# Second attention of a two-layer kernel: value products issued in twos, maximum tiles placed anew between them

## What is computed

```python
q, k, v = proj(wq, bq), proj(wk, bk), proj(wv, bv)      # (B, 16, L, 8), L = 1024
scores = jnp.einsum('bhqd,bhkd->bhqk', q, k) / np.sqrt(HEAD_DIM)
attn = jax.nn.softmax(scores + bias[None], axis=-1)     # bias by relative position
out = jnp.einsum('bhqk,bhkd->bhqd', attn, v)
```

## Time and profile before

| | us |
|---|---|
| median of 3 runs (lowest, highest) | 2570.04 (2569.20, 2572.35) |
| the profiled execution | 2569.28 |
| its span, first to last instruction | 2567.5 |
| TensorE matmuls busy | 2312.1 (90%) |
| VectorE busy | 1850.8 (72%) |
| ScalarE busy | 1497.5 (58%) |
| TensorE busy with attends, L1360 | 267.7 |
| VectorE busy with maxima, L1462 | 605.2 |
| ScalarE busy with exponents, L1444 | 506.2 |

### The profile page before, as it was taken

How to read it: one execution, slowest core, us unless ns; L and a number is a source line. 1 busy time by engine, 2 the same in 40 slices (tenths; PEclk the granted TensorE clock), 3 DMA queues, 4 the chain that set the end, 5 groups by cost and what they waited for, 6 DMA issues and landing times. The chain is left out here.

```text
span 2567.5 us, 46435 instructions
## 1 busy us (share of the span) xinstructions
PE 2312.1 (90%) x17339; PEld 1338.3 (52%) x17339; DVE 1850.8 (72%) x2346; ACT 1497.5 (58%) x2293; POOL 125.4 (5%) x256
## 2 busy tenths in 40 slices
PE   3799999999999999999999955859999999999998
PEld 2466666666565666666566632624444444444444
DVE  8677777777777777777777775067777777777781
ACT  3465666657575656666575731306666566566666
POOL 0100000000000000000000021000000000000000
PEclk8899999999999999999999977959999999999999
DMA  2000000000000000000000008033111110112000
GB/s 75 1 0 0 0 0 0 0 0 0 0 0 0 0 0 0 0 0 0 0 0 0 0 17 194 11 45 63 18 18 20 34 26 18 27 19 32 12 2 10
DMA packets 41099, 41.16 MB, mean 16 GB/s; under 512 B 21392, under 2 KB 33632, under 8 KB 40864
## 3 DMA queue, kind: packets, MB, share of 16 engines
q1 hardware_dynamic: 38904, 36.87, 7.2%
q10 hardware_dynamic: 1448, 1.61, 0.4%
q0 software_dynamic: 640, 1.15, 0.4%
HBM read 26.60 MB, written 11.63 MB: 15 GB/s over the span
## 5 line engine op out<-in xcount | busy, mean ns | idle before, releaser
L1462 DVE TENSOR_REDUCE nm_half<-slot 128x2 f32<-128x1024 f32 x512 | 605.2, 1223 | 188.4 <-PE slot L1311 146.2
L1444 ACT ACTIVATE pT<-slot 128x1024 f32<-128x1024 f32 x512 | 506.2, 1027 | 332.0 <-PE slot L1394 278.7
L573 ACT ACTIVATE probT<-slot 128x1024 f32<-128x1024 f32 x192 | 171.0, 890 | 326.9 <-PE slot L474 326.9
L474 PEld LDWEIGHTS slot<-ident,prob 128*128 128x128 f32 x2304 | 245.7, 141 | 198.6 <-issue 166.8
L610 DVE TENSOR_REDUCE negmax<-slot 128x1 f32<-128x896 f32 (+7 forms) x416 | 282.5, 708 | 76.4 <-PE slot L464 76.4
L474 PE MATMUL slot<-ident,prob 128*128 128x128 f32 x2304 | 328.0, 281 | 2.1
L486 PE MATMUL yspace<-probT,v_sb 128*64 128x512 f32 (+3 forms) x1536 | 318.3, 507 | 0.0
L1306 PE MATMUL slot<-ks,qs 48*128 48x512 f32 x1024 | 254.3, 495 | 53.6 <-DMA ks<-rows 29.1
L565 ACT ACTIVATE prob<-slot,negmax 128x896 f32<-128x896 f32 (+7 forms) x416 | 292.6, 720 | 9.6 <-DVE negmax L610 9.6
L1360 PE MATMUL yspace<-pT,v 128*32 128x512 f32 x2048 | 267.7, 604 | 1.7 <-ACT y_raw L1431 0.8
L459 PE MATMUL slot<-k_hi,q_st 128*128 128x512 f32 (+3 forms) x608 | 240.8, 396 | 26.4 <-ACT prob L565 11.4
(11 more groups left out here) (240 smaller groups left out, 3007.8 us busy)
## 6 DMA issues: line engine op xcount, KB each, us to landing
qs<-q_hi SPq DMA_DIRECT2D x64, 64.0 KB
qs<-q_lo SPq DMA_DIRECT2D x64, 64.0 KB
ks<-k_hi SPq DMA_DIRECT2D x60, 64.0 KB
ks<-k_lo SPq DMA_DIRECT2D x60, 64.0 KB
x_tok<-in_L_attn_x_dram SPq DMA_DIRECT2D x4, 512.0 KB, 7.4
q_hi<-qk_out SPq DMA_DIRECT2D x4, 512.0 KB, 3.2
q_lo<-qk_out SPq DMA_DIRECT2D x4, 512.0 KB, 4.1
k_hi<-qk_out SPq DMA_DIRECT2D x4, 512.0 KB, 4.2
```

Of the source, the lines that this page charges most:

```text
L474: last = nc.tensor.transpose(ps[:, a * BANK + j * P:a * BANK + (j + 1) * P], prob[a][:, p_at(4 * c + j, kt)], ident[:, :])
L1444: nc.scalar.activation(pT[hp][m % PT_DEEP][:, :, :], slot[at["x", n] % RING][:, :].rearrange("p (j t) -> p j t", t=BANK), ACT.Exp)\
L1462: nc.vector.tensor_reduce(nm_half[:, h, :, p * TPB + i], slot[pos % RING][:, :].rearrange("p (a t) -> p a t", t=BANK), AX.X, ALU.max, nega ...
```

## The change

The two lists are replaced, and maximum tasks that were split around an attend now all stand ahead of it:

```diff
-                M_BEFORE = [1, 1, 1, 3, 0, 1, 1, 1, 1, 1, 1, 0, 1, 0, 1, 0, 0, 2, 2, 1, 1, 0, 1, 2, 2, 2, 2, 1, 2, 0, 0, 0]
-                AV_BEFORE = [0, 0, 0, 1, 0, 0, 1, 0, 0, 1, 0, 1, 0, 1, 0, 1, 0, 1, 1, 1, 0, 0, 0, 0, 1, 1, 1, 0, 1, 0, 0, 0]
+                M_BEFORE = [1, 2, 2, 0, 1, 1, 1, 0, 2, 0, 1, 1, 1, 1, 1, 1, 3, 0, 1, 1, 1, 1, 1, 1, 1, 1, 2, 1, 1, 1, 0, 0]
+                AV_BEFORE = [0, 0, 0, 0, 0, 0, 0, 0, 2, 0, 2, 0, 0, 0, 0, 0, 2, 0, 2, 0, 0, 0, 2, 0, 0, 0, 2, 0, 0, 0, 0, 0]
...
                             if not last:
-                                next_maxima(m_before(n)[:1])
+                                next_maxima(m_before(n))
                             for m in av_before(n):
                                 attend(m)
-                            if not last:
-                                next_maxima(m_before(n)[1:])
```

## The result

The changed kernel takes 2674.53 us (median of 4 runs, 2671.98 to 2680.13) against 2569.62 us for the kernel before in the same comparison: a ratio of 1.041, 95% interval 1.0398 to 1.0423. The forecast was 2623 us with a range to 2655. The sign was right, the size was not: +105 us in place of +53.

The account below looks back on a forecast made before the run. TensorE was taken as the bound, with new waits on the three-slot PSUM ring outweighing the pairs' saving. Twelve ordinary quads +45.7, three batch-end quads +8.4, last quad -1.3: +52.8 on 2569.3, plus 0.8, gives 2623 us, range 2596 to 2655.

Parts of the forecast that it names:

- half-clock case: Clock halves from m11 to the end of A5 in each quad: 4 us more a quad, near 2680 us; chance 9%.
- dense stretch: x10 to m18, between the second and third attend pairs: 7.97 us for 5.05 us of TensorE's work, 2.9 us waiting.

Follow-up runs that it names:

- m_only: Against the kernel before, only the maxima are placed as in the changed kernel; attends stand singly at their old places, three in the tail: 2641.6 us, ratio 1.0288.

## What to carry to other kernels

Grouping like matmuls saves about 0.25 us a group here (0.14 in the pair and 0.1 at its border), but a lone long group of matmuls between short tasks is also what lets the readers of a small PSUM ring catch up. Count how many ring tasks stand between two such gaps: with three slots, three tasks went without a stop here and four stopped TensorE for 0.65 us each round. If a change creates a stretch in which TensorE stops before every task, treat the granted clock as part of the change and not as a constant, and price the half-clock case from the start. Cheap matmuls into an idle bank are a test that separates waiting from clock, and on a kernel that cannot be reordered they can be a remedy; where the clock was whole anyway they cost 36 us.

## What was not expected of the hardware

- The granted clock fell although TensorE never stood idle for long: its longest stop in the dense stretch ahead of the fall is 0.52 us (the row at 2165.03 has it), and 0.60 us ahead of the second (a score pair at 2180.21). It went to 0.50 for 6.8 us and again for 3.4 us in each ordinary quad.
- In m_only TensorE stops 0.65 us in every 3.2 us and the clock stays 1.00 (rows above). The difference to see is an attend in each round; stops alone did not bring the clock down. Which of the differences decides is not shown.
- More work made the program faster: 16 useless matmuls a quad, 57 us less.
